# Graph attention's edge pass: column numbers and softmax weights read from a PSUM bank, and another order of VectorE's work

## The chip, the cores and the metric

The kernel runs on one core of a Trainium2 chip. The metric is the device time of one execution in microseconds (us); three executions of the kernel before took 4457.46, 4462.18 and 4467.36 us, so its median is 4462.18 us.

## The reference

Nodes (6250, of 256 features) and 100,000 directed edges sorted by destination go through two layers of multi-head attention over edges, each followed by a feed-forward block, and then through one feed-forward block for the half of the nodes that score highest. The part that matters here is the attention of a layer (8 heads of 32 features):

```
scores = einsum('ehd,ehd->eh', q[dst], k[src]) * scale
m  = segment_max(scores, dst);  ex = exp(scores - m[dst])
z  = segment_sum(ex, dst)
agg = segment_sum((ex / z[dst])[:, :, None] * v[src], dst)
```

## The kernel before

The program plans the edges once, makes queries, keys and values of all nodes, and then runs for each of the two layers an edge pass, a merge of segments that were cut, and a node pass. The change touches the edge pass alone (`edge_pass`).

**Steps and turns.** The edges lie in steps of 128, one edge to a partition. A turn is 8 steps, worked on in 4 pairs m = 0 to 3. A layer has 104 turns, run as a loop with 4 turns in its body. What one turn of edges goes through, with the names that the code and the rows use:

- GpSimd gathers the 512 numbers of key and value of each edge's source node, one indirect DMA a step (L673, into `edge_kv`, which holds 4 turns).
- VectorE makes a one-hot of the destinations from `rel` ("spread", L697). TensorE multiplies it with the queries of a block of nodes (L805): query rows of the edges in PSUM, `edge_q`, two buffers of a pair.
- VectorE multiplies them with the keys ("product", L715) and sums each head ("score", L722).
- After all 4 pairs TensorE turns the scores over (L834, step `score_t`) into the PSUM bank `turned`. VectorE runs a scan forward ("up", L737) and one backward ("top", L744), which give the maximum of each segment; TensorE turns that back (L842, `max_t`) into the same bank.
- VectorE subtracts the maximum ("below", L749) and stores it ("maxima", L750); the two are named "weigh". ScalarE takes the exponential (L909, the weights, into `edge_kv`).
- For each pair VectorE makes a second one-hot ("sel", L758: the column numbers `keep["cols"]` compared with each edge's column in `tab`), and multiplies the values with the weights ("value", L764). TensorE sums the pair's values by segment (L852, `sums`, into PSUM); ScalarE adds each step's sums to its place (L919) and blanks the spent PSUM bank (L920). After pairs 1 and 3 TensorE also makes the sums of cut segments (L863, `ends0` and `ends1`), which ScalarE copies out (L926).

**What sets the order.** Each engine works its instructions off in the order in which they are written. The table `WEAVE` sets this order for a turn on VectorE and TensorE: "product" and "score" belong to the turn itself; "up", "top", "weigh" and "tail" 0 and 1 (sel and value of pairs 0 and 1) to the turn before it; "late" 2 and 3 (pairs 2 and 3) to the one before that. At each "product" TensorE makes query rows two pairs ahead; at "turn", the last entry, it makes `score_t`. The engines tell each other of each step by counting semaphores. Two waits of TensorE matter below: the sums of a pair wait for ScalarE's blanks of the pair before (L848: `acc` of step 2m-1), and `score_t` stands behind pair 1's sums and `ends0` in TensorE's queue.

## Time and profile before

| What | Value |
|---|---|
| Median of 3 executions | 4462.18 us (4457.46 to 4467.36) |
| Span of the profiled execution | 4465.3 us |
| Time of that execution beside its span | within the three times; the span stands 3.1 us above the median |
| Busy: TensorE, VectorE, ScalarE, GpSimd | 82%, 72%, 38%, 46% of the span |
| The two edge passes | slices 5 to 14 and 22 to 31 of 40, where GpSimd is at 7 tenths and the DMA engines at 7 |
| In 500 to 1500 us, inside the first edge pass | TensorE 889.7, VectorE 900.6, ScalarE 550.2, GpSimd 787.3 us busy, granted TensorE clock 1.00 |

The profile is one execution. Busy time of TensorE counts matmuls that overlap each other, so that 889.7 of 1000 us is no bound by itself. VectorE's instructions overlap a little as well: the next one starts before the last has ended, so what an instruction costs is read from its start to the next one's start. GpSimd's busy time is that of the gathers' own instructions, and the stretches of about 0.3 us between two of them are shown as idle.

### The profile page before, as it was taken

The numbers are of one execution on the slowest core, as the hardware profiler recorded it, in microseconds if no ns is written. First come the engines' busy times: TensorE is split into PE (matmuls) and PEld (weight loads), VectorE is DVE, ScalarE is ACT, GpSimd is POOL, SyncE is SP. The second block draws the span as 40 slices with busy tenths as digits, with TensorE's granted clock in tenths as the row PEclk, the third lists the DMA queues.
The fourth block names the chain that finished last, engine by engine and source line by source line (L and its number), as shares of the span: only waits on it lengthen the run. The fifth ranks groups of instructions, "written<-read, shape, count | busy, mean of one in ns | idle before, by whom it ended". The sixth has DMA issues, their size and how long they took to land. (4 is left out here: it accounts for less than half of the span.)

```text
span 4465.3 us, 82525 instructions
## 1 busy us (share of the span) xinstructions
PE 3681.2 (82%) x17048; PEld 2435.5 (55%) x17048; DVE 3232.5 (72%) x7299; ACT 1681.1 (38%) x4755; POOL 2072.2 (46%) x1938
## 2 busy tenths in 40 slices
PE   1777898888998857999988888888888758888488
PEld 1444555555555535777765555455555437777377
DVE  4777899888998865555548998898899766666501
ACT  0111555555555521222214555555555402222021
POOL 2113777777777730000007777777777500000022
PEclk8998999999999978999999999999999979999699
DMA  4224777777777731111117777777777512222011
GB/s 73 85 87 134 214 218 216 212 212 214 218 221 213 219 108 33 48 59 59 59 49 219 217 213 211 207 218 214 213 217 219 170 48 71 82 74 83 23 47 39
DMA packets 357834, 640.43 MB, mean 143 GB/s; under 512 B 107755, under 2 KB 199981, under 8 KB 357594
## 3 DMA queue, kind: packets, MB, share of 16 engines
q0 software_dynamic: 140144, 457.44, 34.7%
q1 hardware_dynamic: 217610, 182.03, 13.9%
q8 instruction: 36, 0.59, 0.1%
q14 instruction: 44, 0.36, 0.0%
HBM read 570.14 MB, written 69.95 MB: 143 GB/s over the span
## 5 line engine op out<-in xcount | busy, mean ns | idle before, releaser
L673 POOL DMA_INDIRECT edge_kv<-kv,edge_idx x1664 | 1871.0, 1124 | 542.1 <-issue 423.0
L852 PE MATMUL edge_sums<-edge_kv,edge_sel 128*128 128x272 f32 x3328 | 979.2, 417 | 142.0 <-ACT edge_sums L920 112.4
L805 PE MATMUL edge_q<-qc,edge_spread 128*128 x3328 | 921.3, 400 | 155.4 <-DVE edge_kv L715 130.4
L919 ACT COPY acc<-edge_sums x1664 | 641.2, 385 | 868.6 <-PE edge_sums L852 704.5
L805 PEld LDWEIGHTS edge_q<-qc,edge_spread 128*128 128x128 f32 x3328 | 580.6, 192 | 430.1 <-issue 374.6
L852 PEld LDWEIGHTS edge_sums<-edge_kv,edge_sel 128*128 128x128 f32 x3328 | 566.6, 190 | 441.8 <-issue 364.2
L715 DVE TENSOR_TENSOR edge_kv<-edge_kv,edge_q 128x512 f32<-128x512 f32 x832 | 564.7, 679 | 242.8 <-DMA edge_kv<-kv,edge_idx 227.2
L920 ACT COPY edge_sums<-edge_blank 128x272 f32 x1664 | 659.6, 396 | 0.0
L764 DVE TENSOR_TENSOR edge_kv<-edge_kv 128x512 f32<-128x512 f32 x832 | 564.4, 678 | 0.9 <-ACT edge_kv L909 0.9
L722 DVE TENSOR_REDUCE edge_score<-edge_kv 128x16 f32<-128x512 f32 x832 | 559.4, 672 | 0.2
L758 DVE TENSOR_TENSOR edge_sel<-cols,edge_tab 128x256 f32<-128x256 f32 x832 | 340.4, 409 | 0.0
L1440 POOL TENSOR_TENSOR middle_rs<-middle_var,middle_power 128x2 f32<-128x2 f32 x50 | 34.5, 690 | 572.5 <-DVE middle_minus_half L1464 572.5
L863 PE MATMUL edge_end_sums<-edge_kv,edge_tab 128*2 128x272 f32 x3328 | 266.9, 392 | 0.0
L1440 POOL TENSOR_TENSOR last_rs<-last_var,last_power 128x2 f32<-128x2 f32 x50 | 34.5, 690 | 479.2 <-DVE last_minus_half L1464 479.2
L1627 PE MATMUL middle_ph<-middle_xt,middle_w 128*128 128x256 f32 x800 | 186.2, 387 | 28.5 <-ACT middle_xt L1705 28.5
L1627 PE MATMUL last_ph<-last_xt,last_w 128*128 128x256 f32 x800 | 182.3, 387 | 27.7 <-ACT last_xt L1705 27.7
L1627 PEld LDWEIGHTS last_ph<-last_xt,last_w 128*128 128x128 f32 x800 | 152.3, 193 | 53.8 <-ACT last_xt L1705 33.9
L1627 PEld LDWEIGHTS middle_ph<-middle_xt,middle_w 128*128 128x128 f32 x800 | 150.3, 193 | 53.3 <-ACT middle_xt L1705 20.4
L1668 PE MATMUL first_ph<-first_w_qkv,first_xt 128*128 128x512 f32 (+1 forms) x400 | 154.0, 544 | 29.3 <-ACT first_xt L1705 29.3
L1637 PE MATMUL last_pp<-last_w,last_hid 128*128 128x256 f32 x800 | 176.8, 379 | 0.0
L1637 PE MATMUL middle_pp<-middle_w,middle_hid 128*128 128x256 f32 x800 | 176.8, 379 | 0.0
L697 DVE TENSOR_SCALAR edge_spread<-edge_rel,part 128x1024 f32<-128x1024 bf16 x208 | 158.9, 764 | 6.3 <-DMA edge_rel<-step_rel 6.3
(367 smaller groups left out, 3974.8 us busy)
## 6 DMA issues: line engine op xcount, KB each, us to landing
edge_rel<-step_rel SPq DMA_DIRECT2D x208, 256.0 KB
edge_kv<-kv,edge_idx POOLq DMA_INDIRECT x1664, 3.8
edge_flags<-step_flags SPq DMA_DIRECT2D x416, 32.0 KB
picked<-last_picked SPq DMA_DIRECT2D x25, 513.0 KB
kv<-first_kv_out SPq DMA_DIRECT2D x25, 512.0 KB
kv<-middle_kv_out SPq DMA_DIRECT2D x25, 512.0 KB
end_rows<-edge_ends SPq DMA_DIRECT2D x416, 8.5 KB
h<-first_h SPq DMA_DIRECT2D x25, 256.0 KB
```

The costliest lines, as they stand in the source:

```text
L673: nc.gpsimd.indirect_dma_start(kv[:, turn[0], j, 0:KV], None, dram["kv"], bass.IndirectOffsetOnAxis(ap=idx[:, turn[0], j:j + 1], axis=0)). ...
L715: dve_p.tick(v.tensor_tensor(k_rows, k_rows, psq[m % QBUFS][:, :, :], ALU.mult), turn, f"product{m}")
L722: dve_p.tick(v.tensor_reduce(score[:, lane, 2 * m * H:2 * (m + 1) * H].rearrange("p (j h) -> p j h", h=H), k_rows.rearrange("p j (h d) -> ...
L758: dve_p.tick(v.tensor_tensor(sel[:, at:at + 2, :], bc(keep["cols"][:, :].unsqueeze(1), [P, 2, P]), bc(tab[:, turn[0], 2 * m:2 * m + 2, 0:1 ...
L764: dve_p.tick(v.tensor_tensor(values, values, bc(kv[:, turn[0], 2 * m:2 * m + 2, KV:KV + H].unsqueeze(3), [P, 2, H, DH]), ALU.mult), turn, ...
L805: mm = t.matmul(psq[m % QBUFS][:, j % 2, :], spread[:, turn[0] % 2, j * P:(j + 1) * P], qc[:, bass.ds(at[j % 2], D)], start=True, stop=True)
L852: pe_p.tick(t.matmul(psa[:, bass.ds(place[j % 2], QC)], sel[:, j, :], kv[:, turn[0], j, D:ROW], start=False, stop=True, skip_group_check=T ...
L863: mm = t.matmul(pse[32 * q:32 * q + 2, 0:QC], tab[:, turn[0], j, 2:4], kv[:, turn[0], j, D:ROW], start=True, stop=True)
L919: s.copy(acc[:, bass.ds(at, QC)], psa[:, bass.ds(bank, QC)])
L920: act_p.tick(s.copy(psa[:, bass.ds(spent, QC)], blank[:, :]), turn, f"acc{j}")
L1627: mm = t.matmul(ph[bank // 2][:, at:at + W * P], mat[:, half, c * P:(c + 1) * P], xt[:, i, half * W * P:(half + 1) * W * P], start=(half = ...
L1637: mm = t.matmul(pp[turn[0]][:, w * D:(w + 1) * D], hid[:, turn[0], at:at + P], mat[:, c, :], start=(c == 0), stop=(c == FF // P - 1))
```

## The change

Four things change in the edge pass:

1. At its start VectorE copies the column numbers into the last 128 columns of the PSUM bank `turned` (`cols`), and "sel" compares from there.
2. ScalarE's exponential runs twice: once into `turned` (`psw`), once into `edge_kv` as before. "value" multiplies with the weights in `psw`.
3. The bank is then read by "sel" and "value", and written by TensorE (`score_t`, `max_t`) and by ScalarE. Waits are added so that a reader and a writer don't meet: pair 3 waits for `max_t` of the turn after its own (`follows`), and pair 0's "sel" waits for the weights, which only its "value" did before.
4. `WEAVE` orders a turn anew, so that "up" comes ahead of "late" 2, and "top" and the product of pair 2 ahead of "late" 3; "tail" 0 and 1 follow each other. "maxima" and "below" change places.

```diff
-CLEARED = 3
+CLEARED = 4
...
-WEAVE = (("product", 0), ("late", 2), ("score", 0), ("up", 0), ("product", 1), ("top", 0), ("late", 3),
...
+WEAVE = (("product", 0), ("score", 0), ("up", 0), ("late", 2), ("product", 1), ("top", 0), ("score", 1),
...
+        psw = turned[:, P + G * H:P + 2 * G * H].rearrange("p (j h) -> p j h", h=H)
+        cols = turned[:, 512 - P:512]
...
+            v.tensor_copy(cols, keep["cols"][:, :]).then_inc(s_clear, 1)
...
+            def follows(turn):
+
+                if turn[1] is not None or turn != LAST_TURN:
+                    pe_p.wait(dve, later(turn, 1), "max_t")
...
-                    dve_p.tick(v.tensor_tensor(below[:, :], score[:, lane, :], psm, ALU.subtract), turn, "below")
                     dve_p.tick(v.tensor_tensor(kv[:, turn[0], :, KV + H:ROW], psm.rearrange("p (j h) -> p j h", h=H),
                                                bc(tab[:, turn[0], :, 1:2], [P, G, H]), ALU.mult),
                                turn, "maxima")
+                    dve_p.tick(v.tensor_tensor(below[:, :], score[:, lane, :], psm, ALU.subtract), turn, "below")
...
+                    if m == PAIRS - 1:
+                        follows(turn)
+                    if m == 0:
+                        act_p.wait(dve, turn, "weights")
                     at = 2 * m
-                    dve_p.tick(v.tensor_tensor(sel[:, at:at + 2, :], bc(keep["cols"][:, :].unsqueeze(1), [P, 2, P]),
+                    dve_p.tick(v.tensor_tensor(sel[:, at:at + 2, :], bc(cols.unsqueeze(1), [P, 2, P]),
                                                bc(tab[:, turn[0], 2 * m:2 * m + 2, 0:1], [P, 2, P]),
                                                ALU.is_equal), turn, f"sel{m}")
-                    if m == 0:
-                        act_p.wait(dve, turn, "weights")
                     values = kv[:, turn[0], 2 * m:2 * m + 2, D:KV].rearrange("p j (h d) -> p j h d", h=H)
                     dve_p.tick(v.tensor_tensor(values, values,
-                                               bc(kv[:, turn[0], 2 * m:2 * m + 2, KV:KV + H].unsqueeze(3), [P, 2, H, DH]),
+                                               bc(psw[:, 2 * m:2 * m + 2, :].unsqueeze(3), [P, 2, H, DH]),
                                                ALU.mult), turn, f"value{m}")
...
-                    act_p.tick(s.activation(kv[:, turn[0], :, KV:KV + H], below[:, :].rearrange("p (j h) -> p j h", h=H),
-                                            ACT.Exp, scale=SCALE), turn, "weights")
+                    less = below[:, :].rearrange("p (j h) -> p j h", h=H)
+                    s.activation(psw, less, ACT.Exp, scale=SCALE)
+                    act_p.tick(s.activation(kv[:, turn[0], :, KV:KV + H], less, ACT.Exp, scale=SCALE), turn, "weights")
```

The order on VectorE from pair 0's "value" to the next "up", across the border of two turns. Before (L764 is "value", L722 "score", L715 "product", L758 "sel", L697 "spread", L737 "up"):

```order
L764 TENSOR_TENSOR edge_kv<-edge_kv 128x2x256
L722 TENSOR_REDUCE edge_score<-edge_kv 128x16
L715 TENSOR_TENSOR edge_kv<-edge_kv,edge_q 128x2x256
L758 TENSOR_TENSOR edge_sel<-cols,edge_tab 128x256
L764 TENSOR_TENSOR edge_kv<-edge_kv 128x2x256
L722 TENSOR_REDUCE edge_score<-edge_kv 128x16
L715 TENSOR_TENSOR edge_kv<-edge_kv,edge_q 128x2x256
L697 TENSOR_SCALAR edge_spread<-edge_rel,part 128x1024
L758 TENSOR_TENSOR edge_sel<-cols,edge_tab 128x256
L764 TENSOR_TENSOR edge_kv<-edge_kv 128x2x256
L722 TENSOR_REDUCE edge_score<-edge_kv 128x16
L737 SCALAR_TENSOR_TENSOR edge_up<-edge_flags,edge_turned 64x128
```

Now, in the same place (the first "value", L774, is pair 0's; "sel" is L770, "score" L725, "product" L718, "spread" L700, "up" L740):

```order
L774 TENSOR_TENSOR edge_kv<-edge_kv,edge_turned 128x2x256
L770 TENSOR_TENSOR edge_sel<-edge_turned,edge_tab 128x256
L774 TENSOR_TENSOR edge_kv<-edge_kv,edge_turned 128x2x256
L725 TENSOR_REDUCE edge_score<-edge_kv 128x16
L718 TENSOR_TENSOR edge_kv<-edge_kv,edge_q 128x2x256
L700 TENSOR_SCALAR edge_spread<-edge_rel,part 128x1024
L725 TENSOR_REDUCE edge_score<-edge_kv 128x16
L740 SCALAR_TENSOR_TENSOR edge_up<-edge_flags,edge_turned 64x128
```

Score 2 and product 3 have moved ahead of pair 0, and "late" 2 behind "up": 10 instructions stood between pair 0's "value" and "up", and 6 stand there now.

The order on TensorE from pair 0's sums to pair 1's. Before (L852 are sums, L805 query rows, L863 the ends; the others set registers):

```order
L852 MATMUL edge_sums<-edge_kv,edge_sel 128x272
L482 TENSOR_LOAD edge_regs_s
L805 ISA
L805 MATMUL edge_q<-qc,edge_spread 128x256
L805 ISA
L805 MATMUL edge_q<-qc,edge_spread 128x256
L116 REGISTER_ALU x2
L852 ISA
L852 MATMUL edge_sums<-edge_kv,edge_sel 128x272
L852 ISA
L852 MATMUL edge_sums<-edge_kv,edge_sel 128x272
L863 MATMUL edge_end_sums<-edge_kv,edge_tab 2x272 x4
```

Now (L862 are sums, L873 the ends, L844 `score_t`):

```order
L862 MATMUL edge_sums<-edge_kv,edge_sel 128x272
L116 REGISTER_ALU x2
L862 ISA
L862 MATMUL edge_sums<-edge_kv,edge_sel 128x272
L862 ISA
L862 MATMUL edge_sums<-edge_kv,edge_sel 128x272
L873 MATMUL edge_end_sums<-edge_kv,edge_tab 2x272 x4
L844 MATMUL edge_turned<-ident,edge_score 64x128
```

The query rows that stood between the two pairs' sums have moved ahead of both.

The order on VectorE from "top" to "weigh". Before (L744 is "top", L749 "below", L750 "maxima"):

```order
L744 SCALAR_TENSOR_TENSOR edge_top<-edge_flags,edge_up 64x128
L758 TENSOR_TENSOR edge_sel<-cols,edge_tab 128x256
L764 TENSOR_TENSOR edge_kv<-edge_kv 128x2x256
L722 TENSOR_REDUCE edge_score<-edge_kv 128x16
L749 TENSOR_TENSOR edge_below<-edge_score,edge_turned 128x64
L750 TENSOR_TENSOR edge_kv<-edge_turned,edge_tab 128x8x8
```

Now (L752 is "top", L757 "maxima", L760 "below"):

```order
L752 SCALAR_TENSOR_TENSOR edge_top<-edge_flags,edge_up 64x128
L725 TENSOR_REDUCE edge_score<-edge_kv 128x16
L718 TENSOR_TENSOR edge_kv<-edge_kv,edge_q 128x2x256
L770 TENSOR_TENSOR edge_sel<-edge_turned,edge_tab 128x256
L774 TENSOR_TENSOR edge_kv<-edge_kv,edge_turned 128x2x256
L757 TENSOR_TENSOR edge_kv<-edge_turned,edge_tab 128x8x8
L760 TENSOR_TENSOR edge_below<-edge_score,edge_turned 128x64
```

Score 1 and product 2 now stand between "top" and pair 3's "sel", and it is this "sel" that first waits for `max_t`, where "below" did.

## Rows read from the trace of the kernel before

**Rows 1.** Busy us by engine, granted clock, DMA share, GB/s, 500 to 1500 us.

```profile
500.00:1500.00 1000.00, 889.72 (x4367) 513.14 (x4359) 900.57 (x1834) 550.23 (x1659) 787.29 (x698) 1.00 0.74 215
```

**Rows 2.** Groups by line, 500 to 1500 us: busy, mean ns | idle before, releasers.

```profile
L673 POOL DMA_INDIRECT edge_kv<-kv,edge_idx x698 | 787.4, 1128 | 212.7 <-issue 176.5 <-PE edge_sums L852 21.6 <-PE edge_end_sums L863 14.6
...
L715 DVE TENSOR_TENSOR edge_kv<-edge_kv,edge_q 128x512 f32<-128x512 f32 x350 | 237.7, 679 | 99.1 <-DMA edge_kv<-kv,edge_idx 96.4 <-PE edge_q L805 1.3 <-issue 0.6
L764 DVE TENSOR_TENSOR edge_kv<-edge_kv 128x512 f32<-128x512 f32 x349 | 236.7, 678 | 0.0
...
L737 DVE TENSOR_TENSOR_SCAN edge_up<-edge_flags,edge_turned 64x128 f32<-64x128 f32 x88 | 35.2, 400 | 0.0
```

**Rows 3.** Timeline, VectorE and GpSimd, 1013 to 1017 us: start, us, engine, instruction.

```profile
1013.02 0.20 DVE L749 TENSOR_TENSOR edge_below<-edge_score,edge_turned 128x64 f32<-128x64 f32 x1
1013.15 0.21 DVE L750 TENSOR_TENSOR edge_kv<-edge_turned,edge_tab 128x64 f32<-128x64 f32 x1
...
1013.28 0.67 DVE L715 TENSOR_TENSOR edge_kv<-edge_kv,edge_q 128x512 f32<-128x512 f32 x1
1013.64 0.95 POOL L673 DMA_INDIRECT edge_kv<-kv,edge_idx  x1 [0.30 <-issue]
...
1013.88 0.41 DVE L758 TENSOR_TENSOR edge_sel<-cols,edge_tab 128x256 f32<-128x256 f32 x1
...
1014.21 0.68 DVE L764 TENSOR_TENSOR edge_kv<-edge_kv 128x512 f32<-128x512 f32 x1
...
1014.82 0.67 DVE L722 TENSOR_REDUCE edge_score<-edge_kv 128x16 f32<-128x512 f32 x1
...
1015.41 0.67 DVE L715 TENSOR_TENSOR edge_kv<-edge_kv,edge_q 128x512 f32<-128x512 f32 x1
...
1016.00 0.41 DVE L758 TENSOR_TENSOR edge_sel<-cols,edge_tab 128x256 f32<-128x256 f32 x1
1016.14 1.70 POOL L673 DMA_INDIRECT edge_kv<-kv,edge_idx  x1 [0.30 <-issue]
1016.34 0.68 DVE L764 TENSOR_TENSOR edge_kv<-edge_kv 128x512 f32<-128x512 f32 x1
```

**Rows 4.** Timeline, VectorE, 1018 to 1023 us.

```profile
1018.13 0.74 DVE L697 TENSOR_SCALAR edge_spread<-edge_rel,part 128x1024 f32<-128x1024 bf16 x1
...
1018.79 0.41 DVE L758 TENSOR_TENSOR edge_sel<-cols,edge_tab 128x256 f32<-128x256 f32 x1
...
1020.33 0.40 DVE L737 TENSOR_TENSOR_SCAN edge_up<-edge_flags,edge_turned 64x128 f32<-64x128 f32 x1
...
1022.52 0.41 DVE L744 TENSOR_TENSOR_SCAN edge_top<-edge_flags,edge_up 64x128 f32<-64x128 f32 x1
...
1022.85 0.39 DVE L758 TENSOR_TENSOR edge_sel<-cols,edge_tab 128x256 f32<-128x256 f32 x1
```

**Rows 5.** Timeline, TensorE and ScalarE, 1015 to 1024 us.

```profile
1015.54 1.18 PE L852 MATMUL edge_sums<-edge_kv,edge_sel 128*128 128x272 f32 x4
...
1016.40 0.39 ACT L919 COPY acc<-edge_sums  x1 [0.68 <-PE edge_sums L852]
...
1016.55 1.03 PE L805 MATMUL edge_q<-qc,edge_spread 128*128 x4
...
1017.56 0.40 ACT L920 COPY edge_sums<-edge_blank 128x272 f32 x1
...
1018.09 1.18 PE L852 MATMUL edge_sums<-edge_kv,edge_sel 128*128 128x272 f32 x4 [0.51 <-ACT edge_sums L920]
...
1019.20 0.64 PE L863 MATMUL edge_end_sums<-edge_kv,edge_tab 128*2 128x272 f32 x8
...
1019.77 0.30 PE L834 MATMUL edge_turned<-ident,edge_score 128*64 128x128 f32 x1
...
1022.73 1.12 PE L805 MATMUL edge_q<-qc,edge_spread 128*128 x4 [0.73 <-DVE edge_kv L715]
...
1023.79 0.27 PE L842 MATMUL edge_turned<-ident,edge_top 64*128 64x64 f32 x1
```

More of the change, by code:

```diff
@@ L447, in _ @@
             nc.vector.tensor_copy(keep["part"][:, :], part_i[:, :])
-WEAVE = (("product", 0), ("late", 2), ("score", 0), ("up", 0), ("product", 1), ("top", 0), ("late", 3),
-         ("score", 1), ("weigh", 0), ("product", 2), ("tail", 0), ("score", 2), ("product", 3), ("tail", 1),
+WEAVE = (("product", 0), ("score", 0), ("up", 0), ("late", 2), ("product", 1), ("top", 0), ("score", 1),
+         ("product", 2), ("late", 3), ("weigh", 0), ("score", 2), ("product", 3), ("tail", 0), ("tail", 1),
          ("score", 3), ("turn", 0))
@@ L537, in edge_pass @@
             dve_steps += [f"product{m}", f"score{m}"]
-        dve_steps += ["up", "top", "below", "maxima"]
+        dve_steps += ["up", "top", "maxima", "below"]
         for m in range(PAIRS):
@@ L769, in _ @@
             groups_of(dve, body)
+            scan_up(LAST_TURN)
             rest(later(LAST_TURN, -1), "late", 2)
-            scan_up(LAST_TURN)
             rest(LAST_TURN, "top", 0)
```

## The prediction

> **What bounds the kernel now.** I read the page's slices first, to find the two edge passes, then the busy time by engine inside one of them, the groups by line there, and at last the timeline of two turns. In 500 to 1500 us TensorE and VectorE both look full at about 0.9 and GpSimd is busy 0.79, at a granted clock of 1.00, so that the clock explains nothing here [rows 1]. The groups say which of them is the limit [rows 2]: the 698 gathers are 787.4 us busy and 212.7 us idle, together 1000.1 us, and nearly all that idle time is the 0.3 us issue gap between two gathers. GpSimd issues without a break. A turn has 8 gathers, so a turn takes 8 x (1128 + 305) ns = 11.46 us, and 1000 us hold 87.25 turns. VectorE waits for gathers at its products, 99.1 us, which is 1.14 us a turn; "up" waits for nothing (0.0 us idle in 88).
>
> What makes a gather long is seen where one meets VectorE [rows 3]. The gather at 1013.64 begins under a product (L715, one operand in PSUM) and takes 0.95 us. The one at 1016.14 begins under "sel" (L758), "value" (L764) follows without a gap until 1017.02, and this gather takes 1.70 us: 0.75 us more, and it ends 0.82 us after "value" does. So a gather stands still while "sel" and "value", both with two operands in SBUF, run, and not under the product. The change gives "sel" and "value" one PSUM operand each, as the product has.
>
> **What the change gives back.** If all gathers take 0.95 us, GpSimd needs 8 x (0.95 + 0.305) = 10.04 us a turn instead of 11.46. VectorE's own work is next. From start to next start [rows 3, 4]: product 0.60 (1013.28 to 1013.88), "sel" 0.33, "value" 0.61, "score" 0.59, scan 0.33 (1022.52 to 1022.85; "up" counted the same), "spread" 0.66, "below" and "maxima" 0.13 each. A turn has 4 products, 4 scores, 4 sels, 4 values, 2 scans, 1 spread and the two small ones: 2.40 + 2.36 + 1.32 + 2.44 + 0.66 + 0.66 + 0.26 = 10.10 us. Nothing in this sum is removed or added by the change. So if VectorE's new order cost nothing, a turn would take 10.1 to 10.3 us (10.3 is 11.46 less the 1.14 of waiting).
>
> **What PSUM operands cost VectorE.** No row has "sel" or "value" with a PSUM operand. The nearest is the product, of the same 128x512 shape: 679 ns with PSUM against 678 for "value" with SBUF alone [rows 2]. I take no cost; 0.01 us an instruction either way keeps the bound, 8 of them being under 0.1 us a turn. The Trainium skill says otherwise: VectorE: DVE Perf Modes, "The TRN2 errata", gives an instruction 120 fixed cycles with a PSUM source and 58 with SBUF, which is an estimated 65 ns more for each of the 8. The pair of rows just named doesn't show it, so the sum leaves it out; what it would make of the time is the second rival below.
>
> **What the order costs.** This is the term that decides. `score_t`, which "up" waits for, stands on TensorE behind pair 1's sums and `ends0`, and pair 1's sums wait for ScalarE to blank what pair 0's sums left. Read once through [rows 5]: pair 0's sums start at 1015.54, ScalarE's first copy at 1016.40, its last blank ends at 1017.96, and pair 1's sums start 0.13 later, at 1018.09, having waited 0.51 us for ScalarE. That is 2.55 us from sums to sums. Then `ends0` at 1019.20, `score_t` at 1019.77, done at 1020.07: another 1.98. From pair 0's sums to the end of `score_t`: 4.53 us, and none of this changes. Add 0.68 for "value" itself and 0.13 to reach TensorE (the product at 1021.91 that ends at 1022.60 releases L805 at 1022.73): 5.34 us after pair 0's "value" starts, "up" can start.
>
> Before, VectorE had 10 instructions to do in that time: from 1014.21 to 1020.33 [rows 3, 4], 6.12 us, so "up" came late enough. Now it has 6: "value" 0, "sel" 1, "value" 1, score 3, product 0, spread, score 0, that is 0.61 + 0.33 + 0.61 + 0.59 + 0.60 + 0.66 + 0.59 = 3.99 us. "Up" is 1.35 us early and waits. Behind it on VectorE stands everything, "late" 2 first, and nobody makes up for it, because the next turn's pair 0 comes a fixed number of VectorE instructions after "up". So "up" to "up" is a closed loop, and its length is the turn.
>
> Walked through, with "up" at 0: "sel" 2 at 0.33, "value" 2 at 0.66, over at 1.34, its sums on TensorE at 1.47. Product 1 at 1.27, "top" 1.87, score 1 2.20, product 2 2.79, and "sel" 3 could start at 3.39. It now waits for `max_t`, and TensorE makes that after the sums of pair 2 and the query rows of pair 3: 1.47 + 1.01 (sums at 1015.54, L805 at 1016.55) + 1.06 (L805 at 1022.73, L842 at 1023.79) + 0.27 = 3.81 [rows 5]. That wait is 0.42 us. "Value" 3 at 4.14, over at 4.82, its sums at 4.95; "maxima" 4.75, "below" 4.88, score 2 5.01, product 3 5.60, "sel" 0 6.20, "value" 0 6.53, over at 7.21, so TensorE could start at 7.34; pair 0's sums also need ScalarE's blanks of pair 3, 4.95 + 2.55 = 7.50. Then + 4.53: `score_t` is done at 12.03, and that is the next "up". VectorE, at 10.52 by its own work, waits 1.51 us there. For the hand-over from TensorE to VectorE and the query rows that stand ahead of pair 0's sums on TensorE I add 0.07: 12.1 us a turn.
>
> Bounds: without the wait for `max_t` and the 0.16 at pair 0's sums the loop is 6.92 + 4.53 = 11.45 us; with 0.3 us more for what the rows don't show (the queue of register loads on TensorE) 12.4. The last turns and first turns of a layer don't close the loop, so of 104 I count 100, twice: 200 x (12.1 - 11.46) = +128 us.
>
> **The rest.** ScalarE's second exponential lies on an engine busy 55% [rows 1], and ends long before "sel" 0: "below" is over at 5.1 and "sel" 0 comes at 6.2, with 0.5 us of exponentials between. Without that cover it would be 0.26 us a turn. "Maxima" ahead of "below" shifts the weights by 0.13 us in the same cover. The copy of the column numbers is one small instruction a layer. On SP and GpSimd nothing is moved; at 12.1 us GpSimd has 2 us to spare, so the gathers run ahead as far as their 4 turns of buffer and the products wait no more. DMA share, 0.74 before, falls with it.
>
> Sum: the profiled span 4465.3 + 128 = 4593; it stands 3 us above the median, so 4590 us.
>
> **The rivals.**
> First, the other side: the loop doesn't bind. Its place is "up", its price 1.51 + 0.42 us, and the point from which it decides is a loop under 11.46 us, 0.64 below the walk. For it: every part of the walk is a single place of the trace, and 11.45, the loop with its two side waits gone, is already there. Against it: the waits are written in the code, and 2.55 us is one pass of four copies on ScalarE that nothing shortens. If the loop fell away wholly, a turn would be 10.1 to 10.3 us and the time 4465 - 200 x 1.2 - 3 = 4222 us; halfway, at 11.1, it would be 4390.
>
> Second, PSUM operands are dearer than the product shows. In the loop stand 6 of the 8 instructions, so 65 ns each makes 12.5 us a turn: 200 x 1.04 gives 4670 us. Against it: 679 and 678 ns.
>
> Third, the change doesn't do what it says, and the gathers stay at 1128 ns. GpSimd's 11.46 us then hides under 12.1 and the time is the forecast's; only if the loop also comes out short is it the time before, 4462 us. The Trainium skill, SBUF — State Buffer, "Who interferes with whom", infers that an instruction of this kind doesn't stop the making of descriptors; by that rule there would be nothing to give back. The 1.70 us gather speaks against it.
>
> **How the numbers follow.** Forecast 0.70, the loop not binding 0.16, dear PSUM operands 0.07, no change 0.07. Within the forecast the loop of 11.5 to 12.4 us gives 4470 to 4650 us. The range also takes in no change and most of the second rival: 4455 to 4670 us, and leaves the fast side out. About 0.2% (9 us) is what a measurement tells from no change. Slower 0.77, same 0.07, faster 0.16.
>
> **What would show it.** Gathers at 0.95 to 1.0 us mean, with GpSimd waiting on TensorE's `ends`; products without a wait for DMA; "up" waiting about 1.5 us a turn on `score_t`, "sel" 3 about 0.4 on `max_t`; "value" still at 0.68 us. The prediction is wrong if "up" doesn't wait, or if "value" grows.

## The result: 5.1% slower, 107 us beyond the forecast

The changed kernel takes 4697.41 us in the median (4693.95 to 4700.35, 4 runs); the kernel before, run beside it on the same chip, 4464.77 us (4457.46 to 4472.93, 4 runs). The ratio is 1.0512, 95% interval 1.0489 to 1.0535. The forecast was slower, 4590 us in a range of 4455 to 4670: the sign was right, and the time lies 27 us above the range.

The changed kernel's busy time by engine from 500 to 1500 us (TensorE's matmuls, its weight loads, VectorE, ScalarE, GpSimd; then granted clock, DMA share and GB/s) answers to [rows 1]:

```profile
500.00:1500.00 1000.00, 797.10 (x4000) 472.12 (x4000) 816.32 (x1681) 516.12 (x1600) 617.49 (x641) 1.00 0.67 197
```

No engine is full any more, at the same granted clock of 1.00. The 641 gathers make 80.1 turns of 8, where there were 87.25: a turn now takes 12.5 us instead of 11.46. VectorE's own work is 816.32 / 80.1 = 10.19 us of it.

The groups by line in the same stretch (busy us, mean ns | idle before, and what ended it) answer to [rows 2]. L675 is the gathers, L862 the sums, L815 the query rows, L774 "value", L718 the product, L770 "sel", L740 "up":

```profile
L675 POOL DMA_INDIRECT edge_kv<-kv,edge_idx x641 | 618.8, 965 | 382.8 <-PE edge_end_sums L873 201.5 <-issue 178.1 <-PE edge_sums L862 3.2
L862 PE MATMUL edge_sums<-edge_kv,edge_sel 128*128 128x272 f32 x1280 | 371.8, 413 | 155.6 <-ACT edge_sums L931 113.0 <-DVE edge_kv L774 30.3 <-issue 7.1
L815 PE MATMUL edge_q<-qc,edge_spread 128*128 x1280 | 350.1, 396 | 47.3 <-issue 47.2
...
L774 DVE TENSOR_TENSOR edge_kv<-edge_kv,edge_turned 128x512 f32<-128x512 f32 x321 | 216.6, 675 | 0.0
L718 DVE TENSOR_TENSOR edge_kv<-edge_kv,edge_q 128x512 f32<-128x512 f32 x320 | 215.5, 673 | 0.0
...
L770 DVE TENSOR_TENSOR edge_sel<-edge_turned,edge_tab 128x256 f32<-128x256 f32 x320 | 131.9, 412 | 33.0 <-PE edge_turned L852 33.0
...
L740 DVE TENSOR_TENSOR_SCAN edge_up<-edge_flags,edge_turned 64x128 f32<-64x128 f32 x80 | 33.0, 412 | 150.7 <-PE edge_turned L844 150.7
```

The bound has changed hands as forecast. Gathers went from 1128 to 965 ns, and GpSimd now waits 201.5 us for TensorE's `ends`. The products no longer wait for gathers (99.1 us before, 0.0 now). In their place VectorE waits at "up" for `score_t` (L844), 150.7 us in 80 turns, 1.88 us each, and at pair 3's "sel" for `max_t` (L852), 33.0 us, 0.41 each. "Value" with a PSUM operand takes 675 ns, as it did without.

One whole turn, from "up" to "up", of 12.49 us, in the timeline of VectorE, TensorE and ScalarE (start us, duration us, engine, instruction, idle before it); L862 are sums, L873 the ends, L930 and L931 ScalarE's add and blank:

```profile
1048.98 0.41 DVE L740 TENSOR_TENSOR_SCAN edge_up<-edge_flags,edge_turned 64x128 f32<-64x128 f32 x1 [1.79 <-PE edge_turned L844]
...
1050.43 1.18 PE L862 MATMUL edge_sums<-edge_kv,edge_sel 128*128 128x272 f32 x4 [0.69 <-DVE edge_kv L774]
...
1052.41 0.27 PE L852 MATMUL edge_turned<-ident,edge_top 64*128 64x64 f32 x1
...
1052.79 0.42 DVE L770 TENSOR_TENSOR edge_sel<-edge_turned,edge_tab 128x256 f32<-128x256 f32 x1 [0.37 <-PE edge_turned L852]
1053.13 0.68 DVE L774 TENSOR_TENSOR edge_kv<-edge_kv,edge_turned 128x512 f32<-128x512 f32 x1
1053.25 1.13 PE L815 MATMUL edge_q<-qc,edge_spread 128*128 x4 [0.57 <-issue]
...
1054.21 1.15 PE L862 MATMUL edge_sums<-edge_kv,edge_sel 128*128 128x272 f32 x4
...
1055.29 0.64 PE L873 MATMUL edge_end_sums<-edge_kv,edge_tab 128*2 128x272 f32 x8
...
1055.86 1.13 PE L815 MATMUL edge_q<-qc,edge_spread 128*128 x4
...
1056.18 0.40 ACT L931 COPY edge_sums<-edge_blank 128x272 f32 x1
...
1056.82 1.17 PE L862 MATMUL edge_sums<-edge_kv,edge_sel 128*128 128x272 f32 x4
...
1058.82 0.40 ACT L931 COPY edge_sums<-edge_blank 128x272 f32 x1
...
1059.45 1.18 PE L862 MATMUL edge_sums<-edge_kv,edge_sel 128*128 128x272 f32 x4 [1.46 <-ACT edge_sums L931]
...
1060.56 0.64 PE L873 MATMUL edge_end_sums<-edge_kv,edge_tab 128*2 128x272 f32 x8
...
1061.13 0.30 PE L844 MATMUL edge_turned<-ident,edge_score 128*64 128x128 f32 x1
...
1061.47 0.41 DVE L740 TENSOR_TENSOR_SCAN edge_up<-edge_flags,edge_turned 64x128 f32<-64x128 f32 x1 [1.91 <-PE edge_turned L844]
```

This is the forecast's walk, and it can be laid beside it step by step, with "up" at 0:

| Step | Forecast | This turn |
|---|---|---|
| pair 2's sums | 1.47 | 1.45 |
| pair 3's "sel", after `max_t` | 3.81 | 3.81 |
| pair 3's sums | 4.95 | 5.23 |
| pair 0's sums | 7.50 | 7.84 |
| pair 1's sums | 10.05 | 10.47 |
| end of `score_t` | 12.03 | 12.45 |
| next "up" | 12.10 | 12.49 |

The walk holds to 0.02 us up to pair 3's "sel", and then loses 0.28 us at one place: pair 3's sums. On the average of the turns that lie in 500 to 1500 us the four sums start 1.50, 5.29, 7.92 and 10.45 us after "up", `score_t` ends at 12.43, and the next "up" comes at 12.5: the loss at pair 3's sums is 0.34 us there.

Ahead of these sums TensorE has the first query rows of the next turn (L815 at 1053.25), which start 0.84 us after `max_t` and wait 0.57 us for nothing that the timeline names. What stands between the two in TensorE's queue is this, in the order of the program:

```
L852 MATMUL edge_turned<-ident,edge_top 128x64
L482 TENSOR_LOAD edge_regs_s
L815 ISA
L815 MATMUL edge_q<-qc,edge_spread 128x256
```

The TENSOR_LOAD fetches the two bank registers of pair 0's sums. A register load isn't counted as busy time, but the trace has it. In 500 to 1500 us (shortest, median and longest in ns, then first and last start):

```profile
L482 PEldq TENSOR_LOAD <-edge_regs_s x320: 532/544/942, 500.4 to 1498.0; - x160
```

In the turn shown this one lasts 545 ns, about as long as the 0.57 us that the query rows wait.

### The profile page after: what moved, and what is told of

Same layout as the page of the kernel before. It is cut to its first block and busy times, and to the rows that moved or that the text cites. A ratio compares the mean times of both kernels' runs of the same rounds, so it can differ in the third digit from the quotient of the medians.

```text
span 4697.2 us, 83049 instructions
## 1 busy us (share of the span) xinstructions
PE 3656.9 (78%) x17048; PEld 2442.3 (52%) x17048; DVE 3215.0 (68%) x7301; ACT 1712.7 (36%) x4963; POOL 1811.1 (39%) x1938
## 5 line engine op out<-in xcount | busy, mean ns | idle before, releaser
L675 POOL DMA_INDIRECT edge_kv<-kv,edge_idx x1664 | 1609.3, 967 | 986.1 <-PE edge_end_sums L873 478.1
L862 PE MATMUL edge_sums<-edge_kv,edge_sel 128*128 128x272 f32 x3328 | 972.5, 415 | 418.8 <-ACT edge_sums L931 297.8
L815 PE MATMUL edge_q<-qc,edge_spread 128*128 x3328 | 918.6, 399 | 134.7 <-issue 115.6
L930 ACT COPY acc<-edge_sums x1664 | 642.7, 386 | 1005.3 <-PE edge_sums L862 866.7
L862 PEld LDWEIGHTS edge_sums<-edge_kv,edge_sel 128*128 128x128 f32 x3328 | 566.1, 190 | 748.7 <-issue 669.7
L815 PEld LDWEIGHTS edge_q<-qc,edge_spread 128*128 128x128 f32 x3328 | 583.3, 191 | 341.4 <-issue 281.5
L931 ACT COPY edge_sums<-edge_blank 128x272 f32 x1664 | 657.9, 395 | 0.0
L718 DVE TENSOR_TENSOR edge_kv<-edge_kv,edge_q 128x512 f32<-128x512 f32 x832 | 560.6, 674 | 17.5 <-DMA edge_kv<-kv,edge_idx 13.1
L774 DVE TENSOR_TENSOR edge_kv<-edge_kv,edge_turned 128x512 f32<-128x512 f32 x832 | 561.5, 675 | 0.0
L725 DVE TENSOR_REDUCE edge_score<-edge_kv 128x16 f32<-128x512 f32 x832 | 558.5, 671 | 0.3
L770 DVE TENSOR_TENSOR edge_sel<-edge_turned,edge_tab 128x256 f32<-128x256 f32 x832 | 343.3, 413 | 87.2 <-PE edge_turned L852 86.2
L740 DVE TENSOR_TENSOR_SCAN edge_up<-edge_flags,edge_turned 64x128 f32<-64x128 f32 x208 | 85.7, 412 | 389.8 <-PE edge_turned L844 386.3
L873 PE MATMUL edge_end_sums<-edge_kv,edge_tab 128*2 128x272 f32 x3328 | 267.8, 393 | 0.0
```

The costliest lines, as they stand in the source:

```text
L675: nc.gpsimd.indirect_dma_start(kv[:, turn[0], j, 0:KV], None, dram["kv"], bass.IndirectOffsetOnAxis(ap=idx[:, turn[0], j:j + 1], axis=0)). ...
L718: dve_p.tick(v.tensor_tensor(k_rows, k_rows, psq[m % QBUFS][:, :, :], ALU.mult), turn, f"product{m}")
L725: dve_p.tick(v.tensor_reduce(score[:, lane, 2 * m * H:2 * (m + 1) * H].rearrange("p (j h) -> p j h", h=H), k_rows.rearrange("p j (h d) -> ...
L770: dve_p.tick(v.tensor_tensor(sel[:, at:at + 2, :], bc(cols.unsqueeze(1), [P, 2, P]), bc(tab[:, turn[0], 2 * m:2 * m + 2, 0:1], [P, 2, P]), ...
L774: dve_p.tick(v.tensor_tensor(values, values, bc(psw[:, 2 * m:2 * m + 2, :].unsqueeze(3), [P, 2, H, DH]), ALU.mult), turn, f"value{m}")
L815: mm = t.matmul(psq[m % QBUFS][:, j % 2, :], spread[:, turn[0] % 2, j * P:(j + 1) * P], qc[:, bass.ds(at[j % 2], D)], start=True, stop=True)
```

## The experiments

Nine more kernels ran, each compared with the kernel before on the same chip. "Turn" is 1000 us divided by a quarter of the products that stand in 500 to 1500 us, and "gather" the mean of one there.

| Kernel | Median us | Ratio to before (95%) | Turn us | Gather ns |
|---|---|---|---|---|
| the change | 4697.4 | 1.0512 (1.0489 to 1.0535) | 12.50 | 965 |
| e1, the order alone | 4684.5 | 1.0497 (1.0474 to 1.0519) | 12.50 | 1260 |
| e2, the change with an order for TensorE | 4315.2 | 0.9668 (0.9648 to 0.9687) | 10.64 | 984 |
| e3, e2 with the operands in SBUF | 4411.4 | 0.9881 (0.985 to 0.9911) | 11.11 | 1087 |
| e4, `score_t` ahead of pair 1's sums | 4530.5 | 1.0147 (1.0116 to 1.0178) | 11.76 | 964 |
| e5, `max_t` ahead of pair 3's query rows | 4816.6 | 1.0786 (1.0754 to 1.0818) | 13.11 | 988 |
| e6, one register load later | 4652.5 | 1.0428 (1.0406 to 1.045) | 12.27 | 981 |
| e7, one copy more on ScalarE | 4770.5 | 1.069 (1.0669 to 1.0711) | 12.86 | 964 |
| e8, e2 with "value" on SBUF | 4334.1 | 0.9698 (0.9666 to 0.973) | 10.75 | 1042 |
| e9, e2 with "sel" on SBUF | 4316.2 | 0.9651 (0.9628 to 0.9674) | 10.67 | 992 |

The theory is the forecast's: the new order closes a loop from "up" to "up" through TensorE and ScalarE, and the operands give the gathers their time back. Its rivals are that the operands themselves cost the time, and that the gathers do.

**e1: the order without the operands.** The new `WEAVE`, with the column numbers, the weights and the waits as they were before (against the change, without the lines that put the waits back):

```diff
-                    dve_p.tick(v.tensor_tensor(sel[:, at:at + 2, :], bc(cols.unsqueeze(1), [P, 2, P]),
+                    dve_p.tick(v.tensor_tensor(sel[:, at:at + 2, :], bc(keep["cols"][:, :].unsqueeze(1), [P, 2, P]),
...
-                                               bc(psw[:, 2 * m:2 * m + 2, :].unsqueeze(3), [P, 2, H, DH]),
+                                               bc(kv[:, turn[0], 2 * m:2 * m + 2, KV:KV + H].unsqueeze(3), [P, 2, H, DH]),
...
-                    s.activation(psw, less, ACT.Exp, scale=SCALE)
```

> The changed order of VectorE and TensorE alone; operands, exponential and waits as before the change (no PSUM operand, no wait of pair 3 for max_t). Theory 'loop': the order closes a loop from 'up' to 'up' through TensorE and ScalarE, so nearly all of the loss is here: 12.3 to 12.5 us a turn, 4660 to 4700 us, 'up' waiting 2.0 to 2.4 us a turn, and gathers longer again (1.05 to 1.2 us mean) without that mattering. Rival 'operands': the loss comes from PSUM operands, their waits and the second exponential; then this kernel stands near the one before, 4440 to 4500 us.

Measured: 4684.5 us and 12.50 us a turn, as expected, and a ratio of 1.0497, with an interval that overlaps the change's own. The gathers, 1260 ns, came out longer than the expected 1.05 to 1.2 us. The groups of e1, gathers, "value" from SBUF and "up":

```profile
L675 POOL DMA_INDIRECT edge_kv<-kv,edge_idx x641 | 807.6, 1260 | 195.3 <-issue 171.5 <-PE edge_sums L859 23.8
...
L771 DVE TENSOR_TENSOR edge_kv<-edge_kv 128x512 f32<-128x512 f32 x320 | 216.0, 675 | 0.0
...
L739 DVE TENSOR_TENSOR_SCAN edge_up<-edge_flags,edge_turned 64x128 f32<-64x128 f32 x80 | 32.9, 412 | 189.6 <-PE edge_turned L841 144.9 <-issue 44.7
```

The whole loss is the order's. The gathers are 295 ns longer than in the change, and it doesn't matter, since "up" sets the turn (80 in 1000 us in both) and waits for TensorE. It is close, though: GpSimd waits for TensorE in only 23.8 of the 1000 us here; that the products of e1 wait 0.0 us shows that it isn't the bound. "Value" takes 675 ns here with both operands in SBUF and 675 ns there with one in PSUM; "sel" takes 404 ns here and 412 there.

One turn of e1 shows something more. L739 is "up", L765 pair 3's "sel", L771 its "value", L812 the query rows, L859 its sums:

```profile
1020.91 0.41 DVE L739 TENSOR_TENSOR_SCAN edge_up<-edge_flags,edge_turned 64x128 f32<-64x128 f32 x1 [2.59 <-PE edge_turned L841]
...
1024.27 0.41 DVE L765 TENSOR_TENSOR edge_sel<-cols,edge_tab 128x256 f32<-128x256 f32 x1
...
1024.61 0.68 DVE L771 TENSOR_TENSOR edge_kv<-edge_kv 128x512 f32<-128x512 f32 x1
...
1025.09 1.13 PE L812 MATMUL edge_q<-qc,edge_spread 128*128 x4 [0.47 <-issue]
...
1026.05 1.15 PE L859 MATMUL edge_sums<-edge_kv,edge_sel 128*128 128x272 f32 x4
```

Pair 3's "sel" doesn't wait for `max_t` here and starts 3.36 us after "up", where the change has 3.81. Its "value" is over at 1025.29, and the sums still start only at 1026.05, behind the query rows. On the average they start 5.30 us after "up", as in the change (5.29). So the wait of pair 3's "sel" isn't on the loop: the loop goes through TensorE's own queue, from `max_t` over the register load and the query rows to pair 3's sums.

**e2 and e3: an order of its own for TensorE.** In e2 everything of the change stays, but TensorE follows a table of its own: `top` (`max_t`) ahead of the query rows of pair 3, the turn's `score_t` ahead of pair 1's sums, and the query rows of the next turn behind pair 3's and behind pair 0's sums. e3 takes e2 and puts operands, waits and exponential back as in e1.

```diff
+PE_WEAVE = (("product", 0), ("late", 2), ("top", 0), ("product", 1), ("late", 3), ("product", 2), ("tail", 0),
+            ("product", 3), ("turn", 0), ("tail", 1))
...
-                for what, m in WEAVE:
+                for what, m in PE_WEAVE:
```

> All of the change, VectorE's order too, but TensorE gets an order of its own: score_t ahead of pair 1's sums, max_t ahead of the query rows of pair 3, the query rows of the next turn between pair 3's and pair 0's sums and between pair 0's and pair 1's. Theory 'loop': score_t no longer waits for ScalarE, 'up' waits next to nothing, gathers of 0.97 us are worth what they give: 10.4 to 10.8 us a turn, 4270 to 4350 us, faster than both. Rival 'operands': TensorE's order doesn't touch the cause and the time stays at 4650 to 4700 us.

> TensorE's own order of the second experiment, with operands, exponential and waits of before the change: the loop is open, and the gathers stand still under sel and value again. Theory 'loop, then gathers': GpSimd is the limit once more, at 8 x (1.10 to 1.15 + 0.305) = 11.2 to 11.6 us a turn: 4420 to 4520 us, products waiting for DMA, 'up' for nothing. Rival: TensorE's order alone is the gain of the second experiment and the operands give nothing; then this kernel is at 4300 to 4340 us too.

Measured: 0.9668 and 0.9881, both faster than before. e2 came as expected (4315.2 us, 10.64 us a turn). e3 came out a little faster than its expected 4420 to 4520 us and 11.2 to 11.6 us a turn: 4411.4 and 11.11, with gathers of 1087 ns where 1.10 to 1.15 us had been expected. Its rival, 4300 to 4340 us, is out. The stretch and the groups of e2 (gathers, product, "sel", "up"):

```profile
500.00:1500.00 1000.00, 926.70 (x4688) 556.92 (x4688) 953.05 (x1970) 605.35 (x1878) 743.66 (x756) 1.00 0.77 232
```

```profile
L677 POOL DMA_INDIRECT edge_kv<-kv,edge_idx x756 | 744.0, 984 | 256.6 <-issue 208.0 <-PE edge_end_sums L875 27.3 <-PE edge_sums L864 21.3
...
L720 DVE TENSOR_TENSOR edge_kv<-edge_kv,edge_q 128x512 f32<-128x512 f32 x376 | 253.6, 674 | 5.9 <-PE edge_q L817 5.7
...
L772 DVE TENSOR_TENSOR edge_sel<-edge_turned,edge_tab 128x256 f32<-128x256 f32 x375 | 154.6, 412 | 41.0 <-PE edge_turned L854 39.9 <-issue 0.9
...
L742 DVE TENSOR_TENSOR_SCAN edge_up<-edge_flags,edge_turned 64x128 f32<-64x128 f32 x93 | 37.1, 399 | 0.0
```

"Up" waits for nothing, and VectorE is the bound: 953.05 us of work, 41.0 of waiting at "sel" and 5.9 at the product make the 1000. What is left of the wait at "sel" is 0.44 us a turn, nearly all of it for `max_t`. The same groups of e3 say what the operands are worth once the loop is gone:

```profile
L677 POOL DMA_INDIRECT edge_kv<-kv,edge_idx x720 | 782.3, 1087 | 219.5 <-issue 194.5 <-PE edge_sums L861 15.5 <-PE edge_end_sums L872 9.4
...
L719 DVE TENSOR_TENSOR edge_kv<-edge_kv,edge_q 128x512 f32<-128x512 f32 x360 | 246.1, 684 | 74.7 <-DMA edge_kv<-kv,edge_idx 69.7 <-PE edge_q L814 1.3
```

Here GpSimd is the bound again: 8 x (1.087 + 0.305) = 11.14 us against a turn of 11.11, and the products wait for gathers. Between e3 and e2 lie 96 us, which is the operands' gain. e2 beats both the kernel before, by 146 us in its own comparison, and the changed one.

**e4 and e5: one step of TensorE each.** e4 is the change with `score_t` ahead of pair 1's sums and nothing else moved; e5 is the change with `max_t` ahead of pair 3's query rows instead. The line that makes TensorE follow the table is as in e2, and the comments name the run:

```diff
+PE_WEAVE = (("product", 0), ("late", 2), ("product", 1), ("top", 0), ("product", 2), ("late", 3), ("product", 3),
+            ("tail", 0), ("turn", 0), ("tail", 1))      # e4
+PE_WEAVE = (("product", 0), ("late", 2), ("top", 0), ("product", 1), ("product", 2), ("late", 3), ("product", 3),
+            ("tail", 0), ("tail", 1), ("turn", 0))      # e5
```

> All of the change; on TensorE one step moves: score_t ahead of pair 1's sums. Theory 'loop': that opens the loop at its long end (2.55 us of ScalarE and 1.68 of sums and ends drop out), 'up' waits no more, and the wait of pair 3 for max_t, behind sums and query rows that now come later after 'up', grows to 1.2 to 1.6 us: 11.3 to 11.7 us a turn, 4440 to 4540 us. Rival: max_t takes the place of score_t wholly and the time stays above 4600 us.

> All of the change; on TensorE one step moves: max_t ahead of the query rows of pair 3. Theory 'loop': pair 3's sel waits no more (0.41 us saved there), but TensorE's queue stands still for 'top', and two groups of query rows now come between max_t and pair 3's sums, so that these start later after 'up' (5.7 to 5.9 instead of 5.2 us) and the whole loop with them: 12.9 to 13.2 us a turn, 4770 to 4850 us, slower than the changed kernel. Rival, waits add up: the 0.41 us saved come off the turn, 12.1 us, 4600 to 4630 us.

Measured: 4530.5 and 4816.6 us, both as expected; e4's turn of 11.76 us is 0.06 longer than expected. "Sel" and "up" of e4, and then the query rows, "sel" and "up" of e5:

```profile
L772 DVE TENSOR_TENSOR edge_sel<-edge_turned,edge_tab 128x256 f32<-128x256 f32 x340 | 139.8, 411 | 123.2 <-PE edge_turned L854 123.2
...
L742 DVE TENSOR_TENSOR_SCAN edge_up<-edge_flags,edge_turned 64x128 f32<-64x128 f32 x85 | 33.9, 398 | 0.0
```

```profile
L817 PE MATMUL edge_q<-qc,edge_spread 128*128 x1221 | 340.8, 401 | 76.7 <-issue 64.3 <-DVE edge_score L727 12.1
...
L772 DVE TENSOR_TENSOR edge_sel<-edge_turned,edge_tab 128x256 f32<-128x256 f32 x305 | 122.5, 402 | 0.0
...
L742 DVE TENSOR_TENSOR_SCAN edge_up<-edge_flags,edge_turned 64x128 f32<-64x128 f32 x76 | 31.3, 412 | 228.1 <-PE edge_turned L846 225.1 <-issue 3.0
```

With `score_t` earlier the wait at "up" is gone, and 0.74 us of each turn with it, but "sel" now waits 123.2 / 85 = 1.45 us for `max_t`. With `max_t` earlier "sel" doesn't wait, and the turn still gets 0.61 us longer: two sets of query rows now stand back to back between `max_t` and pair 3's sums, their unnamed waits come to 64.3 / 76 = 0.85 us a turn (0.59 in the change), and "up" waits 3.0 us. A wait that vanishes is no gain where another place closes the loop. e2 has both steps, and other places for the next turn's query rows besides; the two steps without these were not run.

**e6: the register load moved.** In the change TensorE loads the bank registers of pair 0's sums right behind `max_t`, ahead of the next turn's first query rows. e6 does it at the next "product", behind pair 3's sums (the same lines stand in both branches of "product"):

```diff
-                        ahead_of(turn, m, places, begun)
+                        if m == 3:
+                            ahead_of(turn, 2, places, begun)
+                        if m != 2:
+                            ahead_of(turn, m, places, begun)
```

> All of the change; on TensorE only the load of pair 0's bank registers moves from between max_t and the next turn's first query rows to behind pair 3's sums. Theory 'loop, missing term': my walk of 12.1 us lacked this 0.6 us load, which held the query rows and with them pair 3's sums; without it pair 3's sums start about 0.3 us earlier after 'up', and as everything behind them follows, a turn takes 12.1 to 12.25 us: 4610 to 4650 us. Rival: the load hides under another wait and the time stays within 10 us of 4697.

Measured: 4652.5 us, 2.5 us above the expected 4610 to 4650 and 45 us below the change (38 us by the two ratios, each against its own runs of before). The turn, 12.27 us, is 0.02 above its range. The sums, the query rows and "up" of e6:

```profile
L868 PE MATMUL edge_sums<-edge_kv,edge_sel 128*128 128x272 f32 x1308 | 381.1, 414 | 171.0 <-ACT edge_sums L937 115.9 <-DVE edge_kv L774 45.1 <-DVE edge_sel L770 1.6
L815 PE MATMUL edge_q<-qc,edge_spread 128*128 x1300 | 354.5, 395 | 8.3 <-issue 7.0
...
L740 DVE TENSOR_TENSOR_SCAN edge_up<-edge_flags,edge_turned 64x128 f32<-64x128 f32 x81 | 33.4, 412 | 128.2 <-PE edge_turned L850 99.1 <-issue 29.1
```

The unnamed wait of the query rows falls from 47.3 to 8.3 us, and the turn from 12.50 to 12.27 us. So the load was what held them. On the average pair 3's sums start 5.04 us after "up" instead of 5.29, and all that follows comes earlier by as much (pair 1's sums at 10.22 instead of 10.45). The sums wait for VectorE's "value" instead, 45.1 us where it was 30.3, as the forecast's walk had it.

**e7: the loop made longer.** One copy more on ScalarE, from one spare tile to another, between the two copies of pair 0's second step:

```diff
+        spare = sb("spare", [P, QC])
...
                         s.copy(acc[:, bass.ds(at, QC)], psa[:, bass.ds(bank, QC)])
+                        if j == 1:
+                            s.copy(spare[:, :], blank[:, :])
                         act_p.tick(s.copy(psa[:, bass.ds(spent, QC)], blank[:, :]), turn, f"acc{j}")
```

> All of the change, and one further ScalarE copy of 272 columns (into a tile that nobody reads) between the two copies of step 1 of pair 0, about 0.3 us, right in the hand-over from pair 0's sums to pair 1's. Theory 'loop': it passes into each turn in full: 12.75 to 12.85 us a turn, 4750 to 4775 us, 'up' waiting 0.3 us longer, VectorE's busy time the same. Rival 'operands': ScalarE is about half idle and hides it, 4690 to 4705 us.

Measured: 4770.5 us, as expected, and a turn of 12.86 us, 0.01 above what was expected. About 0.3 us of copying on an engine that is busy 516 of 1000 us comes back as 0.36 us a turn and 73 us in all, at the wait that the loop goes through: the sums wait for ScalarE 135.0 / 78 = 1.73 us a turn, where the change has 113.0 / 80 = 1.41. On the average pair 0's sums start 7.92 us after "up" as in the change, and pair 1's at 10.77 instead of 10.45.

```profile
L863 PE MATMUL edge_sums<-edge_kv,edge_sel 128*128 128x272 f32 x1246 | 363.6, 414 | 177.0 <-ACT edge_sums L934 135.0 <-DVE edge_kv L775 39.9 <-issue 1.7
```

**e8 and e9: which operand gives the gathers their time back.** Both start from e2. e8 lets "value" read its weights from SBUF again, e9 lets "sel" compare with the column numbers in SBUF.

```diff
-                                               bc(psw[:, 2 * m:2 * m + 2, :].unsqueeze(3), [P, 2, H, DH]),
+                                               bc(kv[:, turn[0], 2 * m:2 * m + 2, KV:KV + H].unsqueeze(3), [P, 2, H, DH]),   # e8
-                    dve_p.tick(v.tensor_tensor(sel[:, at:at + 2, :], bc(cols.unsqueeze(1), [P, 2, P]),
+                    dve_p.tick(v.tensor_tensor(sel[:, at:at + 2, :], bc(keep["cols"][:, :].unsqueeze(1), [P, 2, P]),   # e9
```

> As the second experiment, but value reads its weights from SBUF again; sel alone has a PSUM operand. The question is which of the two holds the gathers. If each holds them as long as it runs (value 2.4, sel 1.3 us of a turn), gathers take 1.05 to 1.12 us mean, GpSimd needs 10.8 to 11.4 us, and the time is 4350 to 4470 us. Rival: only sel holds them; then 0.98 us and 4310 to 4330 us as in the second experiment.

> The kernel of e2 (the change with TensorE's own order), in which sel compares with the column numbers in SBUF, as before, and only value reads its weights from PSUM. With both operands in PSUM the gathers took 984 ns on average and the time was 4315 us; with value alone put back to SBUF 1042 ns and 4334 us; with both in SBUF 1087 ns and 4411 us. Theory: each of the two VectorE instructions holds up a gather only while it runs itself with both operands in SBUF, so that here the gathers under sel stretch and those under value do not: 1.03 to 1.07 us on average, and 4325 to 4390 us. Rival: one operand in PSUM is enough, since what counts is the share of VectorE's time without such an instruction: gathers under 1.00 us and 4310 to 4320 us, as in e2.

Measured: 4334.1 us for e8, between the two expectations, and 4316.2 us for e9, where the rival stood: e9 can't be told from e2, and its gathers average 992 ns. Gathers and products of e8, then of e9:

```profile
L677 POOL DMA_INDIRECT edge_kv<-kv,edge_idx x743 | 774.3, 1042 | 226.5 <-issue 194.8 <-PE edge_sums L864 24.7 <-PE edge_end_sums L875 7.0
...
L720 DVE TENSOR_TENSOR edge_kv<-edge_kv,edge_q 128x512 f32<-128x512 f32 x372 | 251.8, 677 | 24.5 <-DMA edge_kv<-kv,edge_idx 20.5 <-PE edge_q L817 2.2 <-issue 0.3
```

```profile
L677 POOL DMA_INDIRECT edge_kv<-kv,edge_idx x757 | 750.8, 992 | 250.5 <-issue 209.8 <-PE edge_sums L864 21.3 <-PE edge_end_sums L875 19.3
...
L720 DVE TENSOR_TENSOR edge_kv<-edge_kv,edge_q 128x512 f32<-128x512 f32 x375 | 252.8, 674 | 6.3 <-PE edge_q L817 6.3
```

In e8 GpSimd still sets the turn, 8 x (1.042 + 0.305) = 10.78 us, and products wait for gathers. In e9 it needs 10.38 us, less than VectorE's turn, and that is why the time is e2's. The theory's forecast for e9 missed: 992 ns is only 8 above e2. Few gathers meet a "sel" there: of the 756 that lie in 500 to 1500 us, 41 last over 1 us and end 0.78 to 0.85 us after a "sel" does, as the held ones below do; their mean is 1.15 us. Single gathers in e9's timeline show the hold itself:

```profile
1003.61 0.68 DVE L776 TENSOR_TENSOR edge_kv<-edge_kv,edge_turned 128x512 f32<-128x512 f32 x1
1003.99 0.95 POOL L677 DMA_INDIRECT edge_kv<-kv,edge_idx  x1 [0.30 <-issue]
...
1008.72 0.75 DVE L702 TENSOR_SCALAR edge_spread<-edge_rel,part 128x1024 f32<-128x1024 bf16 x1
1008.99 1.29 POOL L677 DMA_INDIRECT edge_kv<-kv,edge_idx  x1 [0.30 <-issue]
...
1014.38 0.43 DVE L772 TENSOR_TENSOR edge_sel<-cols,edge_tab 128x256 f32<-128x256 f32 x1 [0.59 <-PE edge_turned L854]
1014.54 1.08 POOL L677 DMA_INDIRECT edge_kv<-kv,edge_idx  x1 [0.30 <-issue]
```

Under a "value" with a PSUM operand a gather takes 0.95 us. Under a "sel" from SBUF it takes 1.08 and ends 0.81 us after "sel" does; under "spread" it takes 1.29 and ends 0.81 us after that.

## Why the prediction was right in kind and short in size

- **The gathers.** Forecast 0.95 to 1.0 us, measured 965 ns. Right, and by the reason given: e1 has 1260 ns with the operands in SBUF.
- **PSUM operands cost nothing.** Forecast so. "Value" takes 675 ns in the change and in e1; "sel" takes 412 ns in the change and in e2, 404 in e1 and 413 in e9 from SBUF. The second rival is out. Its price was also too high by the forecast's own walk: of the six instructions only four lie on the way over ScalarE, which ends last there (7.50 + 0.26 = 7.76 us, against 7.34 + 0.39 = 7.73 on VectorE), so that 65 ns each would have made some 12.36 us a turn and 4640 us.
- **The loop binds.** Right: "up" waits for `score_t`, "sel" for `max_t`, GpSimd for the `ends`. e1 gives the loss to the order, e7 stretches the loop and gets its price back, e2 opens it and the loss becomes a gain. The first rival is out. Its price was too large: the forecast gave 4222 us to a kernel without the loop, and e2 takes 4315, because "sel" keeps 0.44 us of waiting and VectorE's work came to 953.05 / 94 = 10.14 us.
- **The step that failed** is the walk's step from "value" 3, "over at 4.82, its sums at 4.95". It let pair 3's sums start as soon as VectorE was done and put TensorE's own queue ahead of them, a register load and the next turn's first query rows, at nothing. By the turn shown they start at 5.23. The one term for such things, "for the hand-over from TensorE to VectorE and the query rows that stand ahead of pair 0's sums on TensorE I add 0.07", was worked out from no row. What the walk lacked measures 12.49 - 12.03 = 0.46 us: 0.28 at pair 3's sums, 0.06 on the way from there to pair 0's sums, 0.08 on the way to pair 1's, and 0.04 at "up". On the average of the turns it is 0.34, 0.08, nothing and 0.07, so that 0.07 was about right for the hand-over alone. e6 shows that the load makes 0.25 of the 0.34 us at pair 3's sums, and e1 that VectorE isn't what holds them: there "sel" 3 doesn't wait for `max_t`, and these sums start no earlier. So the 0.42 us of that wait, which the forecast counted into the loop and into the first rival's price, is hidden behind TensorE's queue.
- **The price of the load.** The forecast had seen this queue, and put 0.3 us for it, which it read from no row, into the bound of 12.4 instead of into the sum. The Trainium skill, DMA: Bandwidth & Descriptors, "Latency and other measured facts", gives a `tensor_load` a floor of some 600 ns; the trace has 544 ns in the median and 532 at the least, a little under it. That price, looked up for an instruction that the order of the program showed, belonged into the walk.
- **The way to pair 0's sums** was put down to ScalarE, 2.55 us. In the turn shown ScalarE's last blank ends at 1056.58 and the sums start at 1056.82: TensorE's own queue (sums 1.08, `ends1` 0.57, query rows 0.96, together 2.61 us, without a gap) is what ends last. The size was right, the reason wrong.
- **The sum.** 107 us were missing. The turn of 12.49 instead of 12.10 us makes 200 x 0.39 = 78 of them. In the profiled executions the two passes, from the first "up" to the last, take 1286.5 and 1286.6 us, and 1174.5 and 1181.5 before. That is 217 us more, where 128 had been forecast: 89 are missing here, since the first and last turns of a layer, which were not counted, are about as long as the others, and the turn before was 11.44 us rather than 11.46. Some 14 us more lie behind the last "up", 941.0 us against 927.4, and 11 of them behind the edge pass's last instruction, in stages that the change doesn't touch; the mean granted clock of that stretch is 0.89 against 0.91. With one profiled execution of each, it stays open whether they come of the change. The last 4 us were not followed.
- **The range** ended at 4670 us, which stands for a turn of 12.5 us by the second rival. The turn alone would have stayed inside, 4465.3 + 200 x 1.03 - 3 = 4668 us, and for a reason that the forecast didn't have; the turns left out and the 14 us carry the time beyond it.

## What to carry to other kernels

When engines work in written order, a reordering that relieves the busiest of them has to be walked around once, from a step to the same step of the next turn, on every engine's own queue; if that walk is longer than the old bound, the relief is worth nothing until the other engine's order is changed as well. In such a walk every instruction in the queue counts, also those that a profile doesn't list as busy: a register load of half a microsecond sat on this loop. In the timeline it shows only as a wait with no name; its own time stands in the view of the registers that it reads. A cause that frees one engine pays only up to the next bound: with the loop open, the first half microsecond of the operands' gain was enough to hand the bound to VectorE, and e9's half of the edit is as good as the whole.

## What the runs showed of the hardware

- Gathers issued by GpSimd stand still not only under "sel" and "value" with both operands in SBUF, but also under "spread", a TENSOR_SCALAR of 128x1024 with one SBUF tensor: 1.29 instead of 0.95 us in the rows of e9. The Trainium skill, SBUF — State Buffer, "Who interferes with whom", names `tensor_scalar` among the operations that can hold what GpSimd and VectorE share; these rows agree.
- How long the gathers are on average depends on which instructions they meet, and so on the order: with the operands in SBUF 1128 ns before, 1260 in e1 and 1087 in e3, for the same instructions. In 500 to 1500 us, 320 of 640 gathers of e1 last over 1 us, and 59 of 640 in the change.
- A register load in TensorE's queue lasts 544 ns (median of 320 in the change). Where it stood ahead of the next turn's query rows, these waited 47.2 us in 80 turns, 0.59 us each, for nothing that the profile names; with the load behind pair 3's sums (e6) 7.0 us in 81.
